# A second buffer for the turned x, a shared buffer for the exponents of key and query, and a new order of work on every engine, in a chunked linear-attention kernel on one core

## The reference

```
x = x + 0.5 * LN_gain_shift(layernorm(x))        # front: statistics, gain, shift
q, k, v = h @ Wq.T, h @ Wk.T, h @ Wv.T           # h = layernorm(x)
phi = elu + 1                                    # on q and k
S += k v^T ; z += k  (running, causal)           # 16 heads of 32
attn = (q . S) / (q . z + EPS)
x = x + attn @ Wo.T + bo
x = x + 0.5 * LN_gain_shift(layernorm(x))        # back
```

## Time and profile before

| what | value |
|---|---|
| median of 3 runs | 1025.33 us (1024.25 to 1025.99) |
| the profiled execution, its own time | 1025.5 us |
| its span, first to last instruction | 1023.8 us |
| mean granted TensorE clock | 0.962 |
| busy: PE, DVE, ACT, POOL | 89%, 82%, 74%, 70% |

### The profile page before, as it was taken

The page is one execution under the profiler, slowest core; times in us unless marked ns, Lnnn a source line. Parts: engine busy times, 40 slices in busy tenths (PEclk is TensorE's granted clock), DMA queues, the critical chain, the costliest instruction groups (busy, mean ns, idle before and its releaser), DMA issues.

```text
span 1023.8 us, 29832 instructions
## 1 busy us (share of the span) xinstructions
PE 909.5 (89%) x10240; PEld 524.7 (51%) x10240; DVE 837.4 (82%) x1513; ACT 757.8 (74%) x1327; POOL 714.4 (70%) x879
## 2 busy tenths in 40 slices
PE   1468999999999999999999999999999999999974
PEld 1234555555555555555555555555455555555542
DVE  3466988888888888988888889888888888878763
ACT  4367877788777777887777778877777788778761
POOL 1136877867787778777777787777677777767762
PEclk8678999999999999999999999999999999999996
DMA  7145678876666677666666777566577756667872
GB/s 256 21 71 100 133 135 163 166 143 120 141 143 139 138 164 164 145 126 133 139 140 137 163 164 144 123 137 139 126 150 164 161 131 119 137 131 126 142 125 62
DMA packets 421405, 139.81 MB, mean 137 GB/s; under 512 B 402544, under 2 KB 402544, under 8 KB 421360
## 3 DMA queue, kind: packets, MB, share of 16 engines
q1 hardware_dynamic: 421360, 139.24, 66.1%
HBM read 21.76 MB, written 16.78 MB: 38 GB/s over the span
## 4 chain that ended last, share of the span: by engine, by line
PE 57%; DMA 15%; SPq 8%; issue 6%; DVE 6%; ACT 4%; POOL 0%; ACTq 0%; DVEq 0%; POOLq 0%
PE PJ L1125 40%; DMA XT<-XH 14%; PE AV L1198 7%; SPq L333 3%; PE SC L1175 3%; PE AV L1210 3%; PE AV L1195 2%; DVE ATTN L968 2%; PE PJ L1224 2%; DVE TP L949 2%; ACT ATTN L679 1%; SPq L286 1%; SPq L341 1%; SPq L322 1%; ACT DEN L671 1%
## 5 line engine op out<-in xcount | busy, mean ns | idle before, releaser
L1125 PE MATMUL PJ<-wT,XT 128*128 128x512 f16 x2304 | 535.6, 385 | 61.2 <-DMA XT<-XH 51.6
L1125 PEld LDWEIGHTS PJ<-wT,XT 128*128 128x128 f16 x2304 | 217.1, 99 | 320.4 <-DMA XT<-XH 63.1
L472 POOL TENSOR_TENSOR A<-AM,A 128x512 f16<-128x512 f32 x256 | 291.1, 1157 | 12.2 <-ACT A L652 12.2
L652 ACT ACTIVATE A<-AM 128x512 f16<-128x512 f32 x256 | 151.3, 634 | 43.1 <-DVE AM L891 41.6
L1224 PE MATMUL PJ<-wT,AT 128*128 128x512 f16 x768 | 179.0, 383 | 1.6 <-DMA AT<-ATTN 1.6
L464 POOL TENSOR_SCALAR_AFFINE_SELECT AM<-AM 128x512 f32<-128x512 f32 x128 | 81.4, 636 | 105.0 <-ACT AM L642 102.6
L1224 PEld LDWEIGHTS PJ<-wT,AT 128*128 128x128 f16 x768 | 72.9, 99 | 80.2 <-issue 3.5
L1198 PE MATMUL AV<-VN,A 128*128 128x33 f16 x3072 | 112.8, 178 | 0.0
L1195 PE MATMUL AV<-SS,QS 128*128 128x33 f16 x1024 | 109.7, 178 | 3.2 <-POOL A L472 3.2
L1198 PEld LDWEIGHTS AV<-VN,A 128*128 128x128 f16 x3072 | 107.7, 96 | 3.7
L602 ACT ACTIVATE PHI<-PJ,inv_scale 128x512 f32<-128x512 f32 x64 | 43.6, 681 | 79.4 <-PE PJ L1125 79.4
(11 more groups left out here) (98 smaller groups left out, 1529.7 us busy)
## 6 DMA issues: line engine op xcount, KB each, us to landing
X<-in_L_attn_x_dram SPq DMA_DIRECT2D x32, 512.0 KB, 4.2
out_dram<-Y SPq DMA_DIRECT2D x32, 512.0 KB, 4.9
A<-in_L_attn_Wk_dram SPq DMA_DIRECT2D x1, 1024.0 KB, 7.8
A<-in_L_attn_Wq_dram SPq DMA_DIRECT2D x1, 1024.0 KB, 10.1
QS<-in_L_attn_Wv_dram SPq DMA_DIRECT2D x1, 1024.0 KB, 12.2
QS<-in_L_attn_Wo_dram SPq DMA_DIRECT2D x1, 1024.0 KB, 14.4
XT<-XH SPq DMA_TRANSPOSE x64, 4.4
KS<-KN SPq DMA_TRANSPOSE x64, 4.3
```

The costliest lines, as they stand in the source:

```text
L472: g.tensor_tensor(A[:, b, LO, hg], AM[:, k % 4], A[:, b, HI, hg], ALU.subtract).then_inc(a_lo.sem, 1)
L652: a.activation(A[:, b, HI, hg], AM[:, k % 4], ACT.Copy).then_inc(a_hi.sem, 1)
L1125: ins = t_.matmul(PJ[b], XT[:, w, c, b * C:(b + 1) * C], wT[m_][:, m, c, :], start=(c, w, m) == todo[0], stop=(c, w, m) == todo[-1])
```

## The change

Four things change. `XT` becomes two buffers that alternate by chunk, and `turn_x` then waits for the projection of the value two chunks back and not one. `PHI` shrinks from four rows of 512 to two: key and query of one batch share one, so that `exp_relu_q(b)` must wait for `low_k(b)` of the same chunk, and `exp_relu_k(b)` for `phi_q(b)` of the chunk before. The orders of all five engines are written anew. No instruction is added or removed in the steady part and none changes its size.

```diff
-        XT = sb("XT", [P, 2, GROUPS, TOK], F16)
-        PHI = sb("PHI", [P, 4, E])
+        XT = [sb(f"XT{p}", [P, 2, GROUPS, TOK], F16) for p in range(2)]
+        PHI = sb("PHI", [P, BATCH, E])
...
                     def turn_x(b):
-                        if PROJECT:
-                            wait(sp, v_filled, n, b)
+                        if ATTEND:
+                            wait(sp, v_filled, s, b)
...
# exp_relu_k
-                            wait(act, k_lo, s, b)
+                            wait(act, q_phi, s, b)
...
# exp_relu_q
-                        if ATTEND:
-                            wait(act, q_phi, s, b)
-                        a.activation(PHI[:, 2 + b], PJ[b], ACT.Exp, scale=inv_scale[:, 0:1]).then_inc(q_exp.sem, 1)
+                        wait(act, k_lo, n, b)
+                        a.activation(PHI[:, b], PJ[b], ACT.Exp, scale=inv_scale[:, 0:1]).then_inc(q_exp.sem, 1)
...
# body of SyncE
+                prev.next_x()
                 prev.turn_k(0)
                 prev.turn_q(0)
                 prev.turn_attn(0)
-                prev.turn_q(1)
+                prev.turn_k(1)
                 prev.turn_attn(1)
-                prev.next_x()
                 prev.store_y()
                 prev.turn_x(0)
                 prev.turn_x(1)
-                prev.turn_k(1)
+                prev.turn_q(1)
...
# body of TensorE
-                prev.project_q(1)
...
                 now.scores(0, 0)
+                now.scores(0, 1)
+                prev.project_out(0)
                 prev.update(1, 0)
                 prev.update(1, 1)
-                now.scores(0, 1)
-                prev.project_out(0)
...
                 now.attend(0, 0)
                 now.attend(0, 1)
+                now.project_q(1)
...
# body of VectorE, around the front stage
                 prev.attn_low(1)
-                prev.low_k(1)
+                now.front_stats(0)
+                now.front_stats(1)
+                now.front_mean(0)
+                prev.x_low(0)
                 now.front_mean(1)
                 now.mask(0, 0)
-                prev.add_s(1)
-                prev.x_low(0)
                 prev.low_v(1)
                 prev.add_out(0)
                 prev.x_low(1)
+                prev.add_s(1)
```

More of the change, by code:

```diff
@@ L507, in body @@
                 prev.split_a(1, 3)
+                prev.spread_k(1)
+                prev.rstd1_of_x1()
+                prev.split_s(0)
                 prev.spread_q(1)
-                prev.split_s(0)
-                prev.rstd1_of_x1()
                 now.rstd0_of_x()
-                prev.spread_k(1)
                 now.cut(0, 1)
                 now.split_a(0, 0)
+                now.cut(0, 3)
                 now.split_a(0, 1)
-                now.cut(0, 3)
+                now.split_a(0, 2)
                 now.x1_bias()
                 now.rstd2_of_x2()
-                now.split_a(0, 2)
+                prev.split_s(1)
                 now.split_a(0, 3)
                 now.cut(1, 1)
-                prev.split_s(1)
+                now.cut(1, 3)
             first = ops(Step(0, -2))
@@ L693, in body @@
                 opening, following = st.number and st.chunk(0) == -1, st.number and st.chunk(0) == 0
+                prev.sums(0)
                 prev.split_a(1, 0)
-                prev.sums(0)
                 prev.q_half(0)
@@ L703, in body @@
                 prev.attn_half(0)
+                prev.q_half(1)
                 prev.s_half(0)
-                prev.q_half(1)
-                prev.k_half(1)
                 prev.sums(1)
@@ L710, in body @@
                 prev.normalise(0)
-                prev.normalise(1)
                 prev.v_half(1)
                 prev.x_half(0)
+                now.copy_scores(0, 1)
+                prev.normalise(1)
                 prev.x_half(1)
-                now.copy_scores(0, 1)
+                now.split_a(0, 0)
+                now.copy_scores(0, 3)
+                now.split_a(0, 1)
+                now.split_a(0, 2)
+                now.split_a(0, 3)
                 now.front_scale(0)
[L717 to L720, removed]
                 now.front_scale(1)
                 prev.s_half(1)
-                now.split_a(0, 3)
                 now.exp_relu_k(0)
                 now.back_scale(0)
-                now.back_scale(1)
-                now.k_half(0)
                 now.exp_relu_k(1)
@@ L731, in body @@
                 now.copy_scores(1, 1)
+                now.k_half(0)
+                now.k_half(1)
+                now.back_scale(1)
+                now.copy_scores(1, 3)
                 now.exp_relu_q(0)
-                now.copy_scores(1, 3)
             square(0)
@@ L899, in phi_q @@
                         wait(dve, q_relu, n, b)
-                        v.scalar_tensor_tensor(PJ[b], PHI[:, 2 + b], 1.0, PJ[b],
+                        v.scalar_tensor_tensor(PJ[b], PHI[:, b], 1.0, PJ[b],
                                                ALU.min, ALU.add).then_inc(q_phi.sem, 1)
@@ L1022, in body @@
                 opening, following = st.number and st.chunk(0) == -1, st.number and st.chunk(0) == 0
-                prev.phi_q(0)
-                now.front_stats(0)
                 prev.reciprocals(0)
+                prev.front_mean1(1)
+                prev.quotient(0)
                 prev.mask(1, 2)
-                prev.front_mean1(0)
-                prev.quotient(0)
                 prev.low_q(0)
-                prev.front_stats1(1)
-                now.front_mean(0)
                 prev.add_s(0)
+                prev.back_gain(1)
                 prev.phi_q(1)
@@ L1035, in body @@
                     w_low(3)
-                prev.front_mean1(1)
                 prev.attn_low(0)
-                now.front_stats(1)
+                prev.back_y(1)
                 prev.low_q(1)
-                prev.back_y(1)
                 prev.reciprocals(1)
@@ L1052, in body @@
                 prev.x_low(1)
+                prev.add_s(1)
+                now.mask(0, 2)
                 prev.out_stats(0)
-                now.mask(0, 2)
                 prev.add_out(1)
+                prev.out_mean(0)
+                prev.out_stats(1)
                 now.front_gain(0)
-                prev.out_mean(0)
                 now.front_gain(1)
-                prev.out_stats(1)
                 prev.out_mean(1)
                 now.front_x1(0)
+                now.phi_k(0)
                 now.front_x1(1)
-                now.phi_k(0)
                 now.back_gain(0)
-                now.back_gain(1)
                 now.mask(1, 0)
-                now.low_k(0)
-                now.back_y(0)
-                now.front_stats1(0)
                 now.phi_k(1)
@@ L1072, in body @@
                     w_low(2)
+                now.front_stats1(0)
+                now.low_k(0)
+                now.low_k(1)
+                now.front_mean1(0)
+                now.back_y(0)
+                now.front_stats1(1)
+                now.phi_q(0)
             first = ops(Step(0, -2))
```

9 lines of the change are left out of this document (4 added, 5 removed).

## The result

The changed kernel takes 975.01 us (971.21 to 976.51, 4 runs), the kernel before in the same session 1025.66 us: a ratio of 0.9501 (95% interval 0.947 to 0.9531), 5% faster. The forecast was 979, range 971 to 1004. The profiled execution took 976.5 us, its span 974.8.

What follows compares the result with a forecast made beforehand. TensorE was taken as held up by waits for `XT`. Period 27.47 + 0.2 = 27.7 us against 29.30 saves 44.8 us over 28 periods, plus 1.5: 1025.5 - 46.3 = 979.2, so 979, range 971 to 1004.

Steps and rivals of the forecast that it cites:

- The bound and the wait: TensorE: its projections wait for `XT`, 51.6 us in all; without that wait its period is 27.47 us instead of 29.30.
- The load's place: SyncE's queue: with the load gone from ahead, the transpose of x is issued 0.65 us sooner and lands in 4.0, not 5.2.
- The second buffer at nothing: `XT`: the second buffer removes a wait already over for 3 us, so by itself it gives nothing.
- The shared `PHI` and the query's path: ScalarE and VectorE: sharing costs 0; `low_q(0)` keeps 0.2 us spare before `project_v(0)`, batch 1's query 0 to 0.5.
- VectorE's share: VectorE: busy 25.99 us in a period, so 95% full in one of 27.47 us.
- the charge of 0.2 us: Every period: 0.2 us added because some spares of 0.1 to 0.6 us in five places will be missed.
- rival C: Query's path or VectorE: `low_q` 0.5 to 1.2 us late for `project_v`, period 28.0 to 28.7, 988 to 1008 us, chance 0.13.
- The head: The two periods before 141.41: the same wait as in the later ones, 1.5 us more gained.
- The cost of a cold projection: TensorE: two key projections took 7.04 us, not 5.35, after a wait; no such step expected, cost contained in the mean.
- Rivals B and E: `XT`: B, transpose still lands in 5.2 us, 1002 us, chance 0.19; E, issued as late as before, 1025, chance 0.05.
- Rival D: End of SyncE's queue: `scores(1,0)` waits for `turn_q(1)`, which has 0.7 us to spare; slower, 1042 us, chance 0.05.

Runs made afterwards that it cites:

- the load put back: The changed kernel with the load of x back between the last transpose of the attention and the store of y: 1025.9 us.
- the old buffers: The changed kernel's orders with one `XT` and a four-row `PHI`, as in the kernel before: 975.1 us.
- The extra operation: The changed kernel with one more VectorE operation of 0.6 us in each step, right before `low_q(0)`: 985.23 us.
- the load behind the transposes of x: The kernel before with the load of x moved from ahead of the store to right behind both transposes of x: 998.82 us.
- the moved load alone: The kernel before with only the load of x moved, to the head of SyncE's body: 971.09 us.
- the longer loop: The kernel before with the load of x at the head of SyncE's body, and the loop over 26 bodies instead of 24: 971.4 us.

## Why the prediction was right

- **The bound and the wait.** That TensorE waited in the loop only for `XT`, that 27.47 us was its floor, and that the wait would go: shown. The floor measured in the loop is 27.48 in the changed order and 27.41 to 27.45 in the old one.
- **The load's place.** The term was 0.65 us by the issue and 1.3 by the bytes. Measured between the load put back (landing at 29.2 of the period: 554.16 - 524.92) and the changed kernel (27.1): 2.1 us, against 1.95. The two experiments that move the line alone, one each way, show that this is all of the gain in the loop. Of the 1.75 us by which the period fell (29.23 to 27.48) no more could be had, since TensorE then has no wait left. Two readings on the way were off and cost nothing: the ten slices of 350 to 431 GB/s carry 0.81 MB of the 1.05 MB, the rest passes in slower slices beside them; and the loaded row is first read 45 us after its issue in the changed kernel (17 us before), not 20.
- **The second buffer at nothing.** Shown by the old buffers: 975.1 against 975.01.
- **The shared `PHI` and the query's path.** Cost 0, with a spare of 0.2 us named for `low_q(0)`. The extra operation measured 0.15. In the old order 0.5 was named, and it measured 0.5 (0.6 less 0.11). For `low_q(1)` the range "0 to 0.5" was at its low end: its row in the changed kernel ends 0.06 us before `project_v(1)`.
- **VectorE's share.** It was put at 95% of the new period, from a window with 49 instructions, where a step has 46; it is 92% (25.18 of 27.48). The sum did not use it, but the charge of 0.2 us and rival C leant on it.
- **The charge of 0.2 us a period.** This term was mis-sized, by its place. In the loop it is 0: every spare of 0.1 held, in 23 like periods. In the bodies that are written out it is 0.5 to 2.3 us: 29.78, 28.01 and 28.37 us for the three periods from 137.24 on, and 28.21 and 29.41 for the last two. The mean over the 28 periods is (913.14 - 137.24) / 28 = 27.71. That it meets the 27.7 of the sum is luck: the charge was made for missed spares in every period, and what TensorE waited for was landings of `XT` and `AT` outside the loop. The 28 periods gave 820.40 - 775.90 = 44.5 us, where 44.8 were forecast.
- **The head.** This term was mis-sized, and its reason was wrong. The step that began at 141.41 begins at 137.24, 4.2 us sooner, where 1.5 were charged to a wait for `XT` like those in the loop. That and the profiled execution's place 1.5 us above the median make up the difference between 979 and 975. The gain lies further ahead, between the first `project_k(0)` and the third: 41.09 us before, 36.84 us in the changed kernel.

```profile
40.71 7.68 PE L1125 MATMUL PJ<-wT,XT 128*128 128x512 f16 x24 [2.72 <-DMA XT<-XH]
81.80 7.62 PE L1125 MATMUL PJ<-wT,XT 128*128 128x512 f16 x24 [2.90 <-DMA XT<-XH]
```

```profile
41.85 7.94 PE L1124 MATMUL PJ<-wT,XT 128*128 128x512 f16 x24 [2.70 <-DMA XT<-XH]
78.69 8.30 PE L1124 MATMUL PJ<-wT,XT 128*128 128x512 f16 x24 [2.48 <-DMA XT<-XH]
```

  It belongs to the new orders and not to the load: this distance is 36.5 to 37.3 us in all five kernels that have them, the load put back and the old buffers among them, and 38.3 to 41.1 us in the eight that have the old orders or only a piece of the new. Which of the new orders gives it was not found.
- **The cost of a cold projection.** None of the looped steps shows a `project_k` pair of 7.04 us any more, as expected; before, there were two, at 727.16 and 904.98, each after a wait of some 2 us, and the mean granted clock was 0.79 over the 8 us from 727 and from 904.
- **Rivals B and E** did not come: the transpose of x lands in 3.9 us and not in 5.2, and is issued 0.7 us sooner.
- **Rival D.** Its mechanism is real, with other names: the last transpose of SyncE's queue is the next to be late. The prediction gave it 0.7 us to spare in the changed order; it has 1.4 (31.2 against 32.65), since it is issued at 26.8 and not at 27.7. With the old order and the load moved the last one is the key's, and it has 0.7 (it lands at 4.5 of the next period and is wanted at 5.2). A load or a store put ahead of that one uses the spare up and costs 0.6 to 1.1 us a step. What failed there is the expectation of the load behind the transposes of x, which took the next transpose as safe.
- **Rival C** did not come, but the dose of 0.6 us shows how near it was: the new order has given the query's path 0.35 us less spare, and got for it 0.3 us for `XT` (issued at 23.2 and not 23.5), which nothing needs.

Left open: the changed kernel lies 4 us above the moved load alone (0.9501 against 0.9478, intervals that overlap). In the traces 1 us of it is the loop (27.48 against 27.43) and most of the rest lies in the written-out bodies, where the changed kernel's periods are 28.0 to 29.8 against 27.4 to 28.9. Two of these us are the last period alone: 29.41 in the changed kernel, 29.0 to 29.5 in all five kernels with its orders, 27.41 with the load moved alone. The transpose that it waits for lands in 5.5 or 5.6 us in those five, and in 3.6 with the load moved alone. Which part of the new order does that was not found.

## What to carry to other kernels

When a DMA on a shared queue is late by a microsecond or two, look first at what is issued ahead of it that nobody needs soon: moving one load of 512 KB, first read 17 us after its issue, gave all the 5% here, and the second buffer gave nothing, since the wait it took away had been over for 3 us. But the bytes have to pass somewhere: moved to a stretch in which the queue idled they were free, moved two places down they made the next transpose late and cost half the gain. And a busy share tells little of what a further operation costs: the same 0.6 us on an engine that is 92% full cost 10 us at one place and nothing at another, as the distance to the next reader said.

## What was not expected of the hardware

In the written-out bodies the same transpose of x lands much later than in the loop. The changed kernel, the transpose issued at 160.7, and the traffic from there to 167.0 (40 slices, with the queues that carried it):

```profile
XT<-XH SPq DMA_TRANSPOSE x1, 6.3
...
GB/s 202 200 370 345 377 390 364 260 234 403 403 270 159 203 218 229 215 190 260 204 332 205 28 8 7 8 8 197 5 0 0 0 3 10 7 11 10 146 78 286
...
q8 instruction: 1, 0.02, 1.8%
q14 instruction: 1, 0.01, 0.4%
```

For about 2.3 us, but for one slice, nearly nothing moves, while two DMAs of instructions fall in the window; the landing takes 6.3 us where it takes 3.9 in the loop. From 0 to 245 us there are 28 such DMAs of instructions, and from 245 to 845 none.

The kept traces say more than this one window. Take the transpose of x of batch 0 in the eleven runs in which the load does not lie directly ahead of it whole (all but the kernel before and the load put back), issued from 130 to 250 us or behind 830. In 52 cases no DMA of instructions was under way between issue and landing, and they landed in 3.0 to 4.2 us. In 39 cases one was, and they took 3.0 to 6.3; every landing above 4.2 is among them. The step that the longer loop took out of the written-out bodies fits in: 4.7 us with such DMAs, 3.2 without. So the late landings go with the DMAs of instructions, in each of these traces. Whether the one causes the other, and why some transposes with such a DMA under way land in time, no run here isolates.
